# Full attention on one core: every third addition of the row sums by an accumulating DMA

## The reference, cut to what matters

```python
attn = jnp.einsum('bnhd,bmhd->bhnm', q * scale, k)
attn = jax.nn.softmax(attn + bias[None], axis=-1)
out = jnp.einsum('bhnm,bmhd->bnhd', attn, v).reshape(Bw, Nw, Cd)
```

## Time and profile before

| | us |
|---|---|
| median of three executions | 6507.51 |
| lowest, highest | 6507.16, 6508.6 |
| the profiled execution | 6517.03 |
| its span | 6515.1 |

### The profile page before, as it was taken

How to read it: one execution, slowest core, us unless ns; L and a number is a source line. 1 busy time by engine, 2 the same in 40 slices (tenths; PEclk the granted TensorE clock), 3 DMA queues, 4 the chain that set the end, 5 groups by cost and what they waited for, 6 DMA issues and landing times. The chain is left out here.

```text
span 6515.1 us, 122324 instructions
## 1 busy us (share of the span) xinstructions
PE 5921.2 (91%) x37810; PEld 3470.1 (53%) x37810; DVE 4386.3 (67%) x8624; ACT 3220.7 (49%) x6628; POOL 4313.3 (66%) x1449
## 2 busy tenths in 40 slices
PE   2777767769999999999999999999999999987899
PEld 2666645545555555555555555555555555533566
DVE  2666633337777778777777777777777777737540
ACT  1444421113666666666666666666666666651222
POOL 0222222234888888888888888888888888874453
PEclk9999989987999999999999999999999999997899
DMA  1111134442100110110110011011011000014432
GB/s 40 41 41 45 43 110 158 158 165 58 34 26 24 34 34 16 35 47 17 34 31 26 24 35 35 21 43 34 16 34 31 25 16 23 14 38 126 121 94 40
DMA packets 216264, 323.65 MB, mean 50 GB/s; under 512 B 42228, under 2 KB 181078, under 8 KB 212694
## 3 DMA queue, kind: packets, MB, share of 16 engines
q1 hardware_dynamic: 200670, 295.36, 15.8%
q0 software_dynamic: 12432, 19.38, 1.5%
q10 hardware_dynamic: 2664, 2.62, 0.2%
HBM read 179.54 MB, written 137.35 MB: 49 GB/s over the span
## 5 line engine op out<-in xcount | busy, mean ns | idle before, releaser
L1193 DVE TENSOR_REDUCE tops<-ps_m 128x1 f32<-128x448 f32 (+1 forms) x5600 | 3120.2, 618 | 906.6 <-PE ps_m L1096 856.5
L1169 ACT ACTIVATE prob<-ps_s 128x448 f32<-128x448 f32 (+1 forms) x5600 | 2613.6, 548 | 1749.4 <-PE ps_s L1032 1707.5
L1002 POOL TENSOR_TENSOR tile_sum<-prob 128x1792 f32<-128x1792 f32 x448 | 1803.5, 4026 | 658.3 <-ACT prob L1169 658.0
L1032 PE MATMUL ps_s<-queries,keys 97*128 97x448 f32 (+1 forms) x5600 | 2196.9, 397 | 15.3 <-ACT prob L1169 7.5
L1096 PE MATMUL ps_m<-keys,queries 96*128 96x448 f32 (+1 forms) x5600 | 2090.5, 380 | 35.7 <-DMA keys<-k_parts 20.6
L1002 POOL TENSOR_TENSOR tile_sum<-tile_sum,prob 128x1792 f32<-128x1792 f32 x448 | 1808.0, 4036 | 31.8
L1032 PEld LDWEIGHTS ps_s<-queries,keys 97*128 97x128 f32 (+1 forms) x5600 | 1041.4, 187 | 1156.3 <-ACT prob L1169 662.2
L1048 PE MATMUL ps_o<-prob,values 128*32 128x448 f32 x11200 | 1342.3, 551 | 3.0 <-ACT prob L1169 1.2
L1096 PEld LDWEIGHTS ps_m<-keys,queries 96*128 96x128 f32 (+1 forms) x5600 | 1061.3, 190 | 240.5 <-DVE tops L1193 84.5
L257 POOL TENSOR_TENSOR logit<-logit,top 112x896 f32<-112x896 f32 x112 | 188.6, 1684 | 559.5 <-DVE top L374 559.5
L1048 PEld LDWEIGHTS ps_o<-prob,values 128*32 128x32 f32 x11200 | 226.5, 108 | 379.5 <-issue 245.0
(11 more groups left out here) (174 smaller groups left out, 4361.7 us busy)
## 6 DMA issues: line engine op xcount, KB each, us to landing
queries<-q_parts SPq DMA_DIRECT2D x288, 160.0 KB, 3.3
keys<-k_parts SPq DMA_DIRECT2D x96, 392.0 KB, 6.9
xT<-in_x SPq DMA_DIRECT2D x56, 224.0 KB, 2.5
window_out<-oT SPq DMA_DIRECT2D x56, 224.0 KB, 2.0
aT<-window_out SPq DMA_DIRECT2D x56, 224.0 KB, 3.7
hidden<-h SPq DMA_DIRECT2D x28, 448.0 KB, 4.4
q_parts<-hi SPq DMA_DIRECT2D x56, 224.0 KB, 1.9
q_parts<-lo SPq DMA_DIRECT2D x56, 224.0 KB, 2.0
```

Source lines behind the costliest of these rows:

```text
L1002: nc.gpsimd.tensor_tensor(tile_sum[k % 2][:, :, :], left, prob[:, t % SLOTS, :, :], ALU.add).then_inc(summed, 1)
L1032: mm = nc.tensor.matmul(o[:, 0:CH], keys[x.u][:, j, at:at + k], queries[x.v][:, j, own:own + CH], start=True, stop=not last, skip_group_ch ...
L1169: nc.scalar.activation(prob[0:k, t % SLOTS, j, :], ps_s[0:k, score_bank(x.hm, i), 0:CH], ACT.Exp).then_inc(exp_done, 1)
L1193: nc.vector.tensor_reduce(tops[0:rows, j, r - blocks[0], c:c + 1], ps_m[0:rows, e % MB, 0:CH], AX.X, ALU.max).then_inc(m_used, 1)
```

## The change

- `TRIPLES` takes the place of `SUM_TILES`. The tiles are numbered so that the 64-key tile is now the last (t = 24) and the 24 large ones form eight triples (0,1,2) ... (21,22,23). Even triples go to `tile_sum0`, odd ones to `tile_sum1`, and each buffer runs on through four triples of the half.
- In the first triple of each buffer GpSimd adds the first two tiles; in the others it adds the first and the second tile to the buffer. The third tile of every triple is added by a DMA that GpSimd issues, with `accum_op=ALU.add`, from `prob` to `tile_sum`, 128 partitions x 1792 floats (896 KB). So a half has 14 additions and 8 such DMAs in place of 16 additions.
- `total` has 3 items a half in place of 9: `tile_sum0` (at score 99 of the half), the 64-key tile and `tile_sum1` (both at score 11 of the next half). The first and the last wait for the buffer's last DMA (`moved_in`), not for an addition.
- ScalarE's wait for a slot whose tile was a third one is for the DMA's landing.
- GpSimd's DMA waits for the addition before it and for the third tile's exponentials; its additions in a buffer wait for that buffer's last DMA.
- SP sends the shifts of pair 1 ahead of the output's store. The product with the reciprocal stays after the addition of tile 21, which is now the first of the last triple.
- One memset less in the setup; its place is taken by old data of the slot, against zeros in `ones` and `values`.

```diff
-SUM_TILES = [(1, 2, 3, 4)] + [(t, t + 1, t + 2) for t in range(5, 23, 3)] + [(23, 24)]
+TRIPLES = [(t, t + 1, t + 2) for t in range(0, KT - 1, 3)]
...
-        SUMS = len(SUM_TILES)
-        D_ITEMS = SUMS + 1
+        D_ITEMS = 3
...
-        ADDS = [len(tiles) - 1 for tiles in SUM_TILES]
-        ADDS_HALF = sum(ADDS)
+        ADDS_HALF = 2 * len(TRIPLES) - 2
+        MOVES_HALF = len(TRIPLES) // 2
...
+                if x.has_next:
+                    shifts(y, 1)
                 if x.has_before:
                     store(half_before(x))
-                if x.has_next:
-                    shifts(y, 1)
...
-                for k, tiles in enumerate(SUM_TILES):
-                    if x.has_before or k > 1:
-                        pool.wait_ge(d_used, ONE + x.h * D_ITEMS + (k if k > 1 else k - 1))
-                    for before, t in zip(tiles, tiles[1:]):
-                        pool.wait_ge(exp_done, ONE + x.h * TILES + HG * (t + 1))
-                        left = prob[:, before % SLOTS, :, :]
-                        if before != tiles[0]:
-                            pool.wait_ge(summed, ONE + x.h * ADDS_HALF + n)
-                            left = tile_sum[k % 2][:, :, :]
-                        nc.gpsimd.tensor_tensor(tile_sum[k % 2][:, :, :], left, prob[:, t % SLOTS, :, :],
+                for k, (first, second, third) in enumerate(TRIPLES):
+                    total = tile_sum[k % 2][:, :, :]
+                    if k < 2:
+                        if x.has_before:
+                            pool.wait_ge(d_used, ONE + x.h * D_ITEMS - 2 * (1 - k))
+                        pool.wait_ge(exp_done, ONE + x.h * TILES + HG * (second + 1))
+                        nc.gpsimd.tensor_tensor(total, prob[:, first % SLOTS, :, :], prob[:, second % SLOTS, :, :],
                                                 ALU.add).then_inc(summed, 1)
                         n += 1
-                        if t == NORMALIZE_AT and x.has_before:
-                            normalize(x.h - 1, 1 - x.v)
+                    else:
+                        pool.wait_ge(moved_in[k % 2], 16 * (x.h * MOVES_HALF + k // 2))
+                        for t in (first, second):
+                            pool.wait_ge(exp_done, ONE + x.h * TILES + HG * (t + 1))
+                            if t == second:
+                                pool.wait_ge(summed, ONE + x.h * ADDS_HALF + n)
+                            nc.gpsimd.tensor_tensor(total, total, prob[:, t % SLOTS, :, :], ALU.add).then_inc(summed, 1)
+                            n += 1
+                            if t == NORMALIZE_AT and x.has_before:
+                                normalize(x.h - 1, 1 - x.v)
+                    pool.wait_ge(summed, ONE + x.h * ADDS_HALF + n)
+                    pool.wait_ge(exp_done, ONE + x.h * TILES + HG * (third + 1))
+                    nc.gpsimd.nop(nofuse=True)
+                    nc.gpsimd.dma_start(total, prob[:, third % SLOTS, :, :], accum_op=ALU.add).then_inc(moved_in[k % 2], 16)
...
                 if k == 0:
                     pe.wait_ge(den_kept, ONE + x.h)
-                else:
-                    pe.wait_ge(summed, ONE + x.h * ADDS_HALF + sum(ADDS[:k]))
+                if k != 1:
+                    pe.wait_ge(moved_in[k // 2], 16 * MOVES_HALF * (x.h + 1))
...
-            bursts[HG * 4 + 3].append((total, 0, False))
-            for k, tiles in enumerate(SUM_TILES):
-                i = HG * tiles[-1] + 15
+            for k, last in ((0, TRIPLES[-2][-1]), (1, TRIPLES[-1][-1]), (2, TRIPLES[-1][-1])):
+                i = HG * (last + 1) + 12
                 while not bursts[i % TILES]:
                     i += 1
-                bursts[i % TILES].append((total, k + 1, i >= TILES))
+                bursts[i % TILES].append((total, k, i >= TILES))
...
-                    if t > SLOTS:
-                        act.wait_ge(summed, ONE + x.h * ADDS_HALF + added(t - SLOTS))
-                    elif t == SLOTS:
-                        act.wait_ge(d_used, ONE + x.h * D_ITEMS + 1)
-                    elif x.has_before:
-                        act.wait_ge(summed, ONE + (x.h - 1) * ADDS_HALF + added(t + KT - SLOTS))
+                    if t >= SLOTS or x.has_before:
+                        h, user = (x.h, t - SLOTS) if t >= SLOTS else (x.h - 1, t + KT - SLOTS)
+                        triple, place = divmod(user, 3)
+                        if user == KT - 1:
+                            act.wait_ge(d_used, ONE + h * D_ITEMS + 2)
+                        elif place == 2:
+                            act.wait_ge(moved_in[triple % 2], 16 * (h * MOVES_HALF + triple // 2 + 1))
+                        else:
+                            act.wait_ge(summed, ONE + h * ADDS_HALF + added(user))
```

More of the change, by code:

```diff
@@ L798, in full_attention @@
         shift_in = [sem(f"shift_in{p}") for p in range(2)]
+        moved_in = [ctx.enter_context(nc.semaphore(f"moved_in{a}")) for a in range(2)]
         o_kept, den_kept, recip_done, out_ready = sem("o_kept3"), sem("den_kept"), sem("recip_done"), sem("out_ready")
@@ L867, in keys_of @@
         def keys_of(t):
-            return (0, FIRST) if t == 0 else (FIRST + 128 * (t - 1), 128)
+            return (0, FIRST) if t == KT - 1 else (FIRST + 128 * t, 128)
         def entry_of_turn(s, p):
@@ L873, in added @@
         def added(t):
-            n = 0
-            for tiles, adds in zip(SUM_TILES, ADDS):
-                if t in tiles:
-                    return n + max(1, tiles.index(t))
-                n += adds
+            k, place = divmod(t, 3)
+            return k + 1 if k < 2 else 2 * k - 1 + place
         @block.sync
@@ L892, in load_values @@
                 cols = slice(x.g * HG * DH, (x.g + 1) * HG * DH)
-                sp.dma_start(values[x.u][0:FIRST, 0, :], d.v_rows[x.b, 0:FIRST, cols]).then_inc(v_in[x.u], 16)
-                sp.dma_start(values[x.u][:, 1:KT, :],
+                sp.dma_start(values[x.u][0:FIRST, KT - 1, :], d.v_rows[x.b, 0:FIRST, cols]).then_inc(v_in[x.u], 16)
+                sp.dma_start(values[x.u][:, 0:KT - 1, :],
                              d.v_rows[x.b, FIRST:N, cols].rearrange("(t p) c -> p t c", p=128)).then_inc(v_in[x.u], 16)
@@ L1029, in score @@
                 o = ps_s[0:k, score_bank(x.hm, i), :]
-                last = t == KT - 1 and x.s == 0
+                last = t == KT - 2 and x.s == 0
                 own = (CH * x.s) % BLK
@@ L1055, in total @@
                     pe.wait_ge(den_kept, ONE + x.h)
-                else:
-                    pe.wait_ge(summed, ONE + x.h * ADDS_HALF + sum(ADDS[:k]))
+                if k != 1:
+                    pe.wait_ge(moved_in[k // 2], 16 * MOVES_HALF * (x.h + 1))
                 for j in range(HG):
-                    moving = prob[:, 0, j, :] if k == 0 else tile_sum[(k - 1) % 2][:, j, :]
-                    mm = nc.tensor.matmul(ps_d[j * DH:(j + 1) * DH, 0:CH], ones[:, int(k > 0), :], moving,
-                                          start=(k == 0), stop=(k == SUMS))
+                    moving = prob[:, (KT - 1) % SLOTS, j, :] if k == 1 else tile_sum[k // 2][:, j, :]
+                    mm = nc.tensor.matmul(ps_d[j * DH:(j + 1) * DH, 0:CH], ones[:, int(k != 1), :], moving,
+                                          start=(k == 0), stop=(k == D_ITEMS - 1))
                 mm.then_inc(d_used, 1)
@@ L1137, in _ @@
                 fill(Half(FIRST_ROUND, 0), e, 0)
-            pe.wait_ge(ones_set, ONE + 5)
+            pe.wait_ge(ones_set, ONE + 4)
             pe.wait_ge(rows_set, ONE + 3)
@@ L1235, in _ @@
             for u in range(2):
-                nc.vector.memset(values[u][FIRST:128, 0, :], 0.0).then_inc(ones_set, 1)
-            nc.vector.memset(prob[FIRST:128, 0, :, :], 0.0).then_inc(ones_set, 1)
+                nc.vector.memset(values[u][FIRST:128, KT - 1, :], 0.0).then_inc(ones_set, 1)
             dve.wait_ge(tops_set, ONE + 2)
```

## The result

| | before | after |
|---|---|---|
| median of four executions, us | 6507.34 | 6820.47 |
| lowest, highest | 6502.55, 6508.6 | 6815.57, 6833.13 |
| ratio (95% interval) | | 1.0485 (1.0472 to 1.0498) |
| span of the profiled execution, us | 6515.1 | 6818.0 |

The change makes the kernel 4.9% slower. I had forecast 6570 us, 1.0% slower, with 8 chances in 10 between 6340 and 6840 us. The direction was right, the size was off by a factor of five: 313 us where I said 63.

A forecast was written before the change was run, and what follows sets the result against it. TensorE set the pace at 76.4 us a half; afterwards a chain through GpSimd and the last landing would, 62.0 + 8.05 + 7.5 = 77.55 us, 62 us more over 56 halves: 6570 us, 8 in 10 between 6340 and 6840.

The forecast's parts named there:

- TensorE's credit: Six fewer items on TensorE at 0.75 us each: 4.5 us a half, 252 us for the program at most.
- The chain that closes: Loop from TensorE's last sum item through GpSimd's additions and DMAs to the last landing: a half takes 62.0 + 7c + d.
- Issue, c = 1.15 us: GpSimd's cost of issuing one accumulating DMA, with waits and no-op; bounds 0.8 to 1.86 us.
- (e): Rival: GpSimd's issues overlap its additions, 7c falls to about 1, a half 71.9 us; counted within another rival's 4%.
- Landing, d = 7.5 us: Time for the half's last accumulating DMA to land, before TensorE goes on; ends 5.0 and 9.9 us.
- Hence 1.5 us more: Surcharge on a 6 us landing for queries' loads and, in four of seven halves, three more of 392 KB.
- TensorE's clock: TensorE's times were taken from rows at clock 1.00; no term for a slower clock was in the sum.
- 77.55: Forecast length of a half in us, 62.0 + 8.05 + 7.5, 1.1 us more than before.
- (d): Rival: dearer issue or an add slower than twice a copy; 6984 to 7260 us; 16% for all above 6720.
- the slots' waits: ScalarE's waits for third tiles' slots: scores stall a microsecond or two, adding nothing while GpSimd is never idle.

The follow-up runs named there:

- e2: Changed kernel with the eight accumulating DMAs of a half left out, GpSimd raising the semaphores itself: 6256.33 us, ratio 0.9617.
- e10: Changed kernel with the keys', corner's and values' loads behind SP's wait for TensorE's last item of the sum: 6636.22 us, ratio 1.0202.
- e4: Changed kernel with the last triple's third tile (tile 23) added by GpSimd, not by a DMA: 6521.86 us, ratio 1.0037.
- e5: e4 with the sum's last item at score 15 of the next half instead of 11, denominators kept after tile 4 instead of 3: 6527.62 us.
- e9: e5 with the even buffer's last item also moved, from score 99 of its own half to score 3 of the next: 6496.05 us, ratio 0.9983.
- e12: e9 with each accumulating DMA moving only the third tile's first two heads, 448 KB instead of 896: 6442.28 us, ratio 0.9905.

## Why the prediction was right and wrong

- **TensorE's credit**: right, 0.74 us an item where I had 0.75; e2 shows 72.0 us a half for 71.9.
- **The chain that closes** over the sum's last item: right in kind. A least-squares line through the 55 times from one last item to the next, against the last DMA's landing in between, has a slope of 1.1 us for each us, and the halves without keys or values and without a slow stretch took 76.8 to 78.3 us.
- **Issue, c = 1.15 us**: measured 1.24. GpSimd idles 0.62 us before the DMA's record, and the next addition's record begins 0.62 us after it starts, before its 0.88 us are over, so there is some of the overlap that I had spoken against in (e). Additions in the run of triples took 8.43 us for two, where I had 8.26.
- **Landing, d = 7.5 us: this is the step that failed**, in the sentence "Hence 1.5 us more". Alone it was well bounded (6.4 us from the start of the record, by rows that gave 5.6 and 9.9), and queries alone add 0.6 us or less in most halves. But I named the keys' three DMAs of 392 KB and then spread them in an average surcharge, and left the values' load (1536 KB) out. Beside the keys the landing takes 12.5 us in 27 halves, beyond my upper end of 9.9, for which I had allowed no company at all; beside the values it takes 10.0 us in 7. The mean is 9.9. Taking this company away (e10) gave back 184 us.
- **TensorE's clock**: a term put at nothing without a reason. I took rows at clock 1.00 although I forecast stalls. From the last item to the DMA of the second triple 11.8 us pass in the 21 halves without a stretch at 1.2 GHz just there and 13.6 us in the other 34; that is 1.1 us a half on average.

The 4.5 us a half between 77.55 and the 82.05 us measured from item to item then split so: the landing 1.7 us (9.9 from the record's start, of which 0.6 already count in the issue, where mine was 7.5), the clock 1.1, additions and issues 1.5, and 0.2 are left over. So the landing is the largest part and not the whole. This split is worked out and not tested; the edits tested the landing with the slow stretches that come of it, and that the clock by itself costs 1.1 us was not shown.

The range held the time, 20 us from its upper end, and that owes something to luck. The time lies where I had put (d), "much slower", at 16%, but neither condition of (d) came true: an issue cost 1.24 us and not 1.86, and the add alone took 1.6 times as long as the plain copy, not more than twice. What made the landing long was company, which stood in no rival. I had also written that the slots' waits add nothing while GpSimd is never idle. That fits the changed kernel, but these waits close rings of their own: with the last landing out of the chain the half is still 75.2 to 76.8 us long (e4, e5, e9, e12), where I had expected 73.5 to 74.6 for the first three.

By the Trainium skill's "DMA: Bandwidth & Descriptors" (the anatomy of one DMA on the software path) and "Collectives: The Full Stack" (the bandwidth ceiling) I had estimated 6.2 us for the accumulating DMA, from 2.0 us plus 2.1 us for each read, which makes 4.1 us for a plain one. This case shows 6.4 and 3.9 us, so both agree within 0.2 us. The estimate was for a DMA alone, and took no account of another load.

## What to carry to other kernels

Where a DMA enters a chain that closes once a loop, price its landing beside every load that can be in flight at that moment, case by case and not as an average: here one landing was 6.4 or 12.5 us, and it set the pace. Take the last step of such a chain by an engine (here 4.2 us in place of 0.6 + 6.4 to 12.5), and use the DMA only for steps whose result is wanted late. After removing one wait look for the buffer that hangs on the same landing; here the next ring was only some 2 us a half shorter (e10, 78.7 us, against e4, 76.7).

## What the runs showed of the hardware

- An accumulating DMA of GpSimd, 128 x 7 KB from SBUF to SBUF, lands 6.4 us after its record's start, a plain one 3.9 us, half the bytes with the add 4.3 us (medians). Beside a load of 3 x 392 KB it lands after 12.5 us on average. Its record on GpSimd is 0.88 us (0.58 plain), the same for half the bytes (e12), and the next addition starts 0.62 us after that record's start.
- The stall of 7.65 us of TensorE shown above was accompanied by a fall to 1.2 GHz: the granted clock is 0.82 and 0.75 as means of 8 us, 1.00 before and after. Without the DMAs (e2) the attention's mean is 1.00, in the changed kernel 0.95.
- The records of GpSimd's additions and product get longer in the changed kernel: the product 1.15 us and 1.42 us after, an addition that follows an issue 4.3 in place of 4.0 us. Records overlap there, though. In the turn shown above the next addition starts 1.10 us after the product, and in one such turn of the kernel before it is 1.11 us (3225.75 to 3226.86); the longer record did not hold the next instruction up. Two additions of a triple do take 8.43 us from start to end, 0.17 us more than at the pace of before.
